# The second norm's row from VectorE to ScalarE, routing one to three steps earlier, constant tables over four steps

## What is computed

```python
# attention: 16 heads of 8, keys and values from ctx, queries from layernorm(x)
x = x + tanh(g_xattn) * attention(layernorm(ctx), layernorm(layernorm(x)))
# experts: 8 routed of which 2 are taken for a token, and 1 shared, F = 256
xn = (x - mean(x)) / sqrt(var(x) + 1e-5)          # the second norm
gates = sigmoid(xn @ Wg)
vals, idx = top_k(gates, 2); vals /= vals.sum()
shared = (silu(xn @ Ws1) * (xn @ Ws3)) @ Ws2
routed = sum over the two experts e of vals * (silu(xn @ We1[e]) * (xn @ We3[e])) @ We2[e]
x = x + tanh(g_ffn) * (shared + routed) / 3
```

## Time and profile before

| | |
|---|---|
| median of three runs | 461.3 us (459.54 to 461.4) |
| profiled execution | 458.93 us, span 457.1 us |
| TensorE busy | 359.4 us (79%) |
| VectorE busy | 344.0 us (75%) |
| ScalarE busy | 264.9 us (58%) |
| GpSimd busy | 279.4 us (61%) |
| mean granted clock of TensorE | 0.915 of full speed |

### The profile page before, as it was taken

How to read it: one execution, slowest core, us unless ns; L and a number is a source line. 1 busy time by engine, 2 the same in 40 slices (tenths; PEclk the granted TensorE clock), 3 DMA queues, 4 the chain that set the end, 5 groups by cost and what they waited for, 6 DMA issues and landing times.

```text
span 457.1 us, 10667 instructions
## 1 busy us (share of the span) xinstructions
PE 359.4 (79%) x3718; PEld 269.3 (59%) x3718; DVE 344.0 (75%) x866; ACT 264.9 (58%) x601; POOL 279.4 (61%) x375
## 2 busy tenths in 40 slices
PE   0689999997998969899869710999999999999400
PEld 0356666665765647676658600777777777778300
DVE  2559999999999998998848820576777777777447
ACT  1257777776687746687656600355555555556244
POOL 3373666666379966888647773017777777777700
PEclk9999999999799988899979865799999999999855
DMA  4920699991001110000001155113236666541179
GB/s 110 275 77 3 261 375 377 391 385 41 13 27 49 36 48 25 27 25 26 25 23 42 49 217 165 52 52 94 93 95 231 232 231 230 210 184 52 47 264 298
DMA packets 39331, 62.36 MB, mean 136 GB/s; under 512 B 5936, under 2 KB 23344, under 8 KB 39280
## 3 DMA queue, kind: packets, MB, share of 16 engines
q1 hardware_dynamic: 32704, 51.12, 32.6%
q0 software_dynamic: 4992, 10.30, 6.7%
q10 hardware_dynamic: 1584, 0.27, 0.4%
HBM read 18.32 MB, written 31.56 MB: 109 GB/s over the span
## 4 chain that ended last, share of the span: by engine, by line
PE 41%; DVE 25%; issue 13%; POOL 13%; ACT 4%; DMA 3%; POOLq 0%; DVEq 0%; SPq 0%; ACTq 0%
POOL expert_rows L545 7%; PE ps L1215 6%; PE ps L1216 5%; PE ps L1217 5%; DVE row_max L935 5%; PE ps L1252 3%; DVE inv_sum L976 3%; PE ps L1158 3%; POOL token_sums L622 3%; PE ps L1112 3%; DVE norm L900 2%; PE ps L1240 2%; PE ps L1238 2%; PE ps L1239 2%; DVE x_sb L1061 2%
## 5 line engine op out<-in xcount | busy, mean ns | idle before, releaser
L622 POOL DMA_INDIRECT token_sums<-prob,y_at x92 | 94.5, 1027 | 60.7 <-DVE prob L1035 38.8
L545 POOL DMA_INDIRECT expert_rows<-c_sb,pos x64 | 64.3, 1005 | 16.9 <-issue 16.8
L587 POOL TENSOR_TENSOR k_mask<-k_st,head_mask 128x512 f32<-128x512 f32 x32 | 33.5, 1046 | 43.8 <-ACT k_st L695 43.6
L739 ACT ACTIVATE h_hi<-prob 128x512 fp32r<-128x512 f32 x62 | 38.3, 634 | 36.5 <-DVE prob L998 36.5
L732 ACT ACTIVATE probT<-ps 128x512 f32<-128x512 f32 x62 | 36.9, 598 | 30.6 <-PE ps L1217 27.0
L1112 PE MATMUL ps<-k_mask,qT 32*64 32x256 f32 x512 | 46.0, 431 | 9.4 <-DVE prob L941 7.7
L998 DVE TENSOR_TENSOR prob<-ps,probT 128x512 f32<-128x512 f32 x62 | 40.2, 684 | 13.9 <-ACT probT L732 10.9
L935 DVE TENSOR_REDUCE row_max<-ps 128x16 f32<-128x1024 f32 x32 | 38.9, 1216 | 11.0 <-PE ps L1112 10.9
L1003 DVE TENSOR_TENSOR h_lo<-prob,h_hi 128x512 fp32r<-128x512 f32 x62 | 40.5, 689 | 3.4 <-ACT h_hi L739 0.4
L1019 DVE TENSOR_TENSOR xT_lo<-ps,xT_hi 128x512 fp32r<-128x512 f32 x23 | 15.9, 692 | 35.9 <-ACT xT_hi L744 35.9
L703 ACT ACTIVATE probT<-ps 128x512 f32<-128x512 f32 x64 | 35.2, 595 | 10.5 <-PE ps L1158 10.4
(11 more groups left out here) (164 smaller groups left out, 977.1 us busy)
## 6 DMA issues: line engine op xcount, KB each, us to landing
expert_rows<-zeros SPq DMA_DIRECT2D x36, 520.0 KB, 5.2
c_sb<-expert_rows SPq DMA_DIRECT2D x23, 260.0 KB, 2.7
wbuf_hi<-w_hi SPq DMA_DIRECT2D x15, 384.0 KB, 2.9
wbuf_lo<-w_lo SPq DMA_DIRECT2D x15, 384.0 KB, 3.4
w_raw<-in_L_ffn_We_dram SPq DMA_DIRECT2D x24, 128.0 KB, 4.2
c_sb<-token_sums SPq DMA_DIRECT2D x8, 256.0 KB, 4.7
xT_lo<-token_sums SPq DMA_DIRECT2D x8, 256.0 KB, 4.9
out_dram<-x_sb SPq DMA_DIRECT2D x8, 256.0 KB, 4.9
```

The source lines that it names most:

```text
L545: pool.indirect_dma_start(out=xs, out_offset=bass.IndirectOffsetOnAxis(pos[:, k, i:i + 1], 0), in_=c_sb[:, i, :], in_offset=None).then_inc ...
L622: pool.indirect_dma_start(out=ys, out_offset=bass.IndirectOffsetOnAxis(y_at[:, s, k:k + 1], 0), in_=yrows[:, s % 2, k * D:(k + 1) * D], in ...
```

## The change

Four things are changed together. The normalised row of the second norm, `(x - mean) * rstd`, is made by ScalarE as `x * rstd + shift`; GpSimd makes `shift = -mean * rstd` after the power. Gates, counts and ranks of the first four groups come one to three steps earlier, and all five parts of `routing` stand in one step. Scatters begin in step 15 and not 18, and after step 37 only tiles 28 to 31 are left. The tables are made in four parts over steps 0 to 3.

```diff
-        GATE_STEP = [14, 22, 30, 34, None]
-        COUNT_STEP = [16, 24, 32, 36, None]
-        RANK_STEP = [17, 25, 33, 37, None]
+        GATE_STEP = [13, 21, 29, 33, None]
+        COUNT_STEP = [14, 22, 30, 34, None]
+        RANK_STEP = [15, 23, 31, 35, None]
...
         def scatter_tiles(t):
-            if 18 <= t < NT:
-                return range(t - 18, t - 17)
-            return {NT: [14], NT + 1: [15], NT + 2: [16, 17], NT + 3: [18, 19], NT + 4: [20, 21],
-                    NT + 5: [22, 23]}.get(t, [])
+            if 15 <= t < NT:
+                return range(t - 15, t - 14)
+            return {NT: [17, 18], NT + 1: [19, 20], NT + 2: [21, 22], NT + 3: [23, 24], NT + 4: [25, 26],
+                    NT + 5: [27]}.get(t, [])
...
-            def tables():
+            def tables(part):
+
                 exact = dict(channel_multiplier=0, allow_small_or_imprecise_dtypes=True)
+                if part == 0:
+                    pool.memset(zeros[:, :], 0.0).then_inc(zeros_set, 1)
...
+                if part == 1:
+                    pool.wait_ge(table_step, 1)
...
+                if part == 2:
+                    pool.wait_ge(table_step, 2)
...
+                if part == 3:
...
+                    pool.iota(slot_less[:, :], [[1, DYN]], base=1 - JMAX, **exact).then_inc(tables_ready, 1)
...
@@ GpSimd, step(t, b) @@
                 i = t - 4
                 if within(i):
                     pool.wait_ge(var2_done, i + 1)
+                    if reused(i):
+                        pool.wait_ge(xn2_ready, i - 1)
                     pool.tensor_tensor(rstd2[:, b:b + 1], var2_eps[:, b:b + 1], minus_half[:, 0, 0:1],
-                                       ALU.pow).then_inc(scale2_ready, 1)
+                                       ALU.pow).then_inc(rstd2_done, 1)
+                    pool.wait_ge(rstd2_done, i + 1)
+                    pool.tensor_scalar(shift2[:, b:b + 1], mv2[:, b, 0:1], rstd2[:, b:b + 1], -1.0, ALU.mult,
+                                       ALU.mult).then_inc(scale2_ready, 1)
...
-                if t == 0:
-                    tables()
+                if 0 <= t < 4:
+                    tables(t)
...
             def unit(n):
-                if n == TAIL_UNIT:
-                    for i in range(24, 28):
-                        scatter(i)
...
@@ ScalarE, step(t, b), between xT_f and w_hi @@
+                i = t - 4
+                if within(i):
+                    act.wait_ge(scale2_ready, i + 1)
+                    act.activation(c_sb[:, i, 0:D], x_sb[:, i, :], ACT.Identity, bias=shift2[:, b:b + 1],
+                                   scale=rstd2[:, b:b + 1]).then_inc(xn2_ready, 1)
...
@@ VectorE, step(t, b) @@
                 for g, last in enumerate(COUNT_STEP):
-                    if last is not None and last - 1 <= t <= last:
-                        for part in (range(0, 3) if t < last else range(3, 5)):
+                    if t == last:
+                        for part in range(5):
                             routing(g, part)
...
-                i = t - 4
-                if within(i):
-                    dve.wait_ge(scale2_ready, i + 1)
-                    dve.tensor_scalar(c_sb[:, i, 0:D], x_sb[:, i, :], mv2[:, b, 0:1], rstd2[:, b:b + 1], ALU.subtract,
-                                      ALU.mult).then_inc(xn2_ready, 1)
...
                     if reused(t - 3):
-                        dve.wait_ge(xn2_ready, t - 4)
+                        dve.wait_ge(scale2_ready, t - 4)
...
@@ TensorE, step(t, b) @@
                 i = t - 6
                 if within(i):
                     pe.wait_ge(xT_f32_ready, i + 1)
+                    pe.matmul(p_logit[:, i, :], xT_f32[:, b, :], wg_raw[:, :], start=True,
+                              stop=True).then_inc(logits_ready, 1)
                     if t > NT and t in GATE_STEP:
                         pe.wait_ge(gate_exp, GATE_STEP.index(t) + 1)
-                    pe.matmul(p_logit[:, i, :], xT_f32[:, b, :], wg_raw[:, :], start=True,
-                              stop=True).then_inc(logits_ready, 1)
...
                     if isinstance(t, int) and t == NT + 1:
                         pe.wait_ge(attn_ready, NT)
+                    if t > NT + 1 and t in RANK_STEP:
+                        pe.wait_ge(pos_ready, RANK_STEP.index(t) + 1)
                     pe.transpose(x2_bank(t), c_sb[:, i, 0:D], ident[:, :]).then_inc(xn2_turned, 1)
```

More of the change, by code:

```diff
@@ L118, in gated_attention_and_experts @@
         rstd2 = sb("rstd2", [P, 2])
+        shift2 = sb("shift2", [P, 2])
         minus_half = sb("minus_half", [P, LB, 2])
@@ L224, in gated_attention_and_experts @@
         var2_done = sem("var2_done")
+        rstd2_done = sem("rstd2_done")
         scale2_ready = sem("scale2_ready")
@@ new lines, in tables @@
+            def tables(part):
+                exact = dict(channel_multiplier=0, allow_small_or_imprecise_dtypes=True)
+                if part == 0:
+                    pool.memset(zeros[:, :], 0.0).then_inc(zeros_set, 1)
+                    pool.wait_ge(zeros_set, 1)
+                    pool.memset(zeros[:, :].rearrange("p (r d) -> p r d", d=XW)[:, :, D:D + 1], NOWHERE).then_inc(zeros_set, 1)
+                    pool.iota(c_sb[:, :, D].rearrange("p (c k) -> p c k", k=CH), [[CT, NC], [1, CH]], base=0,
+                              channel_multiplier=CH, allow_small_or_imprecise_dtypes=True).then_inc(table_step, 1)
+                if part == 1:
+                    pool.wait_ge(table_step, 1)
+                    pool.tensor_scalar(c_sb[:, :, D], c_sb[:, :, D], 1.0 / T, None, ALU.mult)
+                    pool.iota(nowhere[:, :, :], [[ROWS, SLOTS], [1, CH]], base=2 * T, channel_multiplier=CH,
+                              allow_small_or_imprecise_dtypes=True)
+                    pool.memset(ones[:, :], 1.0)
+                    pool.memset(not_before[:, :], -1.0)
+                    pool.memset(earlier[:, :, :], 1.0)
+                    for b in begins.values():
+                        pool.memset(b[:, :], 1.0)
+                    pool.iota(carry[:, 0, :], [[T // P, E]], base=0, channel_multiplier=0,
+                              allow_small_or_imprecise_dtypes=True).then_inc(table_step, 1)
+                if part == 2:
+                    pool.wait_ge(table_step, 2)
+                    pool.affine_select(out=not_before[:, :], in_=not_before[:, :], compare_op=ALU.is_ge, fill=0.0, base=0,
+                                       pattern=[[-1, P]], channel_multiplier=1)
+                    pool.affine_select(out=earlier[:, :, :], in_=earlier[:, :, :], compare_op=ALU.is_ge, fill=0.0, base=-1,
+                                       pattern=[[1, E], [-1, E]], channel_multiplier=0)
+                    for n, t in begins.items():
+                        pool.memset(t[:, :].rearrange("p (e t) -> p e t", e=E)[:, :, 0:1], 0.0)
+                if part == 3:
+                    pool.iota(steps512[:, :, :], [[T, E], [ROWS, JMAX - 1]], base=ROWS, **exact)
+                    pool.iota(slot_id[:, :], [[1, DYN]], base=0, **exact)
+                    pool.iota(slot_less[:, :], [[1, DYN]], base=1 - JMAX, **exact).then_inc(tables_ready, 1)
```

26 lines of the change are left out of this document (removed).

## The result

The changed kernel takes 475.68 us (median of 4 runs, 473.71 to 478.94) where the kernel before, on the same chip, takes 460.42 (459.1 to 461.4): a ratio of 1.034, with a 95% interval of 1.0274 to 1.0407. It is slower by 3.4%. The forecast was 464.1 us and the range ended at 470; the sign was right, the size was not, and the time lies outside the range.

A forecast was written before the change was run, and what follows sets the result against it. VectorE's loop (5.74 us) and a ScalarE-TensorE loop (5.5 us) lay close, with GpSimd's at 6.45 in scatter steps. Attention +4.9, tail +4.0 and backlog -6.1 gave +2.8 us: median 464.1 us, range 456 to 470.

The forecast's parts named there:

- fifteen steps, 13 to 28: Attention steps with the first two groups' routing and scatters: from 101.0 us to 103.4, +2.4 us.
- Two at 5.9, since GpSimd enters them ahead: Two steps after group 0's routing: 5.9 us each, GpSimd's lead hiding its longer loop; then 5.9, 6.4, 7.1.
- The merged routing: All five parts in one step: 9.9, 5.5, 7.6 us for group 0, with a slow-clock step; 10.4 for group 1.
- Nine steps, 4 to 13: Early attention steps before routing: 5.9 us each, 53.1 us in all for 51.9, +1.2 us.
- Tables: Tables in four steps end TensorE's wait before the scores at 32.21 us: gain 0.9 us, no more.
- 28 to 31: Three attention steps with group 2's routing: from 18.7 us to 20.9, +2.2 us.
- The tail: From step 31 to the last places: +4.0 us, between +2.8 and +5.1, TensorE waiting for places in step 35.
- The backlog: Scatters after the last places: only tiles 28 to 31 left, ending 6.1 us before 278.9 without delays.
- Rival 1: ScalarE's row is hidden, steps fall to VectorE's loop of 5.48 us: 455.7 us, chance 0.20.
- Rival 2: The merged routing costs nothing, slow clock covered and places in time for step 35: 457.1 us, chance 0.17.
- Rival 3: GpSimd is later than thought, shift costing 0.54 us and w_lo's wait reaching steps 15 to 25: 469 us, chance 0.18.
- Rival 4: Identity needs a table load beside Silu, two loads each in steps 33 to 35: 471.8 us, chance 0.03.

The follow-up runs named there:

- order experiment: The changed kernel with power and shift ahead of k_mask in GpSimd's step: 468.25 us, 1.0172; the order was also compared with the row alone and with routing split.
- e2_routing: The kernel before with only the earlier, merged routing, its scatters and TensorE's waits; row on VectorE, tables in one step: 473.02 us, 1.0271.
- the fillers: 28 idle identity matmuls on TensorE behind steps 14, 22 and 30, added to the kernel with the earlier, merged routing alone: 466.43 us, 1.0108.
- e1_row: The kernel before with only the ScalarE row and its shift; routing and tables as before: 467.36 us, 1.0166.
- e3_tables: The kernel before with only the tables made in four steps: 458.4 us, 0.9929.
- e6_group3_late: The earlier, merged routing alone, but with the fourth group left in its old steps, in two parts, scatters thinned to match: 470.98 us, 1.0179.
- e7_tail_scatters: The kernel before with tables in four steps and scatters of tiles 14 to 25 packed denser into steps 32 to 37: 453.98 us, 0.9813.
- e5_early_split: The earlier routing alone, with each group's parts split over two steps as before, scatters from step 16: 463.02 us, 1.0008.
- e11_tail_fillers: The kernel before with tables in four steps, denser scatters behind step 31, and 10 idle matmuls before the scores of steps 16 and 24: 455.21 us, 0.9878.

## Why the prediction was wrong

**The failed step: fifteen steps, 13 to 28, at +2.4 us.** They cost 16.5. Two of its assumptions fell.

*"Two at 5.9, since GpSimd enters them ahead", then "5.9, 6.4, 7.1", and behind group 1 "5.9, 6.2, 6.9, 6.1".* The loop itself was sized right: 7.1 us on average over four parts, 6.25 before; measured over the five from k_mask 18 to 23, 7.19 and 6.28. And k_mask to w_lo, 2.82 predicted, was 2.85. What was wrong is where it binds. From the k_mask at 124.03 on, GpSimd waits for k_st only twice in the next eleven (3.54 us behind group 1, 0.17 later), and its loop is paid every time: from k_mask 17 to k_mask 30 are 97.5 us, 86.5 before. The rows of before held the refutation: GpSimd's wait for k_st in a step without scatters is 1.44 us. That is its whole lead. A loop longer by 1.2 us than the others uses it up in about one step; I let it last for four. Besides, the lateness doesn't stay with GpSimd: the row waits for the shift, and exp, v_st, sT, tT and TensorE's k queue behind the row. The waits of 1.96, 1.44 and 1.72 us shown above are that, and behind some of them stands the lower clock. I had written "behind that w_hi" and stopped there. The order experiment prices this at 6.6 to 9.3 us by the ratios, in three settings.

*The merged routing: 9.9, 5.5 and 7.6 for group 0, then 5.9 and 5.9; 10.4 for group 1.* Group 0's three steps came at 10.7, 5.5 and 7.8, close. But these were set against steps of before that I had not added up: its five steps from 13 to 18 take 33.6 us, mine 34.8, and in `e2_routing` 38.9, since the slow step (8.8) and the next (7.2) both ran over. For group 1 the step was 14.0 us and not 10.4; in `e2_routing` 13.1. In the changed kernel two reasons show in the rows: TensorE came into it at the lower clock (157.76), and the routing operation L832 took 1.72 us at 166.79 where its twin at 165.18 took 0.22, beside a scatter and k_mask (167.36) on GpSimd, until that ended. The Trainium skill (SBUF — State Buffer, "SBUF: two separate sides") has a VectorE operation with two SBUF inputs, against a GpSimd operation that reads SBUF, among those that lock the other out or are locked out; L832 is one, and the row agrees. The twin at 165.18, beside a scatter alone (164.98), was not held. Nor is the hold new. The kernel before has one in the same group, beside a scatter and k_mask (162.97) again:

```profile
162.54 1.83 DVE L821 TENSOR_TENSOR gate_tmp<-gate_tmp,rank 128x64 f32<-128x64 f32 x1
```

With it, step 23 of before already took 10.9 us for the same three parts of the routing that step 15 did in 8.9: I priced group 1 from group 0's row when its own was there, 2 us dearer, and put 0.3 for operations held beside GpSimd. The part costs 12 us by the runs, and 7.5 of them go with the fillers: most of it is the lower clock in a step that has nothing to cover it. I named that mechanism and gave it 1.0 us a group.

**Nine steps, 4 to 13.** Predicted +1.2; steps 7 to 13 came at 5.9 to 6.0 us with VectorE idle 0.54. But step 6 took 7.6 us in this run (5.4 or 6.0 in the other kernels with the row), so the stretch was 54.7 us for 51.9. It is one more place of the lower clock, behind a gap of 1.00 us that ended when tT did:

```profile
48.35 0.58 PE L1155 MATMUL ps<-sT,wk_sb 128*128 128x128 f32 x2 [1.00 <-issue]
48.73 1.91 PE L1166 MATMUL ps<-ident,prob 128*128 128x128 f32 x8
```

In `e1_row` the stretch was 53.2 us, for 53.1 in the forecast. ScalarE's row adds 0.40 us to its loop (0.36 taken), and GpSimd's shift 0.26 to 0.38 (0.30 taken).

**Tables.** Predicted -0.9, measured -2.3 at step 4 and -3.3 by the ratio of `e3_tables`. Term mis-sized: I stopped the gain at the gap before the scores, but step 2 as a whole came down from 7.8 to 5.9 us.

**28 to 31.** +2.2 predicted, +2.4 measured.

**The tail.** TensorE was to go on at 30.3 us after the start of step 31: it did at 30.4 (265.83 less 235.41), behind a wait of 3.74 us for the places. The rest of the term was off: the exchange was to give back 1.6 us and the lower clock to take up to 2.3, of which I put about half in. The twelve rows of chunk 3's up-projections, most at 0.63 instead of 0.39 us, took 4.9 us where before they took 2.8, so the clock took 2.1; with TensorE's +4.5 that leaves 0.8 given back and not 1.6. The term is +5.8, not +4.0, above its upper bound of 5.1. `e6_group3_late` shows that this is group 3's move.

**The backlog.** -6.1 predicted, -7.1 measured. The term was mis-sized by one scatter: the row at 277.62 in the earlier trace rows is the last but one of the 28, and the 278.9 that the prediction took for the end of before is where the last one starts:

```profile
278.89 0.95 POOL L545 DMA_INDIRECT expert_rows<-c_sb,pos  x1 [0.30 <-issue]
```

With its end at 280.1 the same working gives -7.4, near what came, and a forecast 1.3 us lower: this slip hid a part of the miss. Most of the gain comes without the moves, in `e7_tail_scatters` (-5.0).

**The rest.** Taken as unchanged; it was 2.0 us longer in the profiled run; the experiments have 177.1 to 180.2. These are single executions, and the cause is open.

**The rivals.** Rival 1 (the row hidden) falls in the early steps, at 5.97 us. With power first the row's whole cost can't be told from none in one setting, is 3.6 us in another. Rival 2 falls: the merge costs 12 us. Rival 3 (GpSimd later than I think) had the right place and the right sign, with too small a price, 5 us over the forecast, and a shift of 0.54 us where it takes 0.26 to 0.38. Rival 4 falls: six table loads before, six after. The signs that the prediction named as right were there (one routing step at 14.0 and not near 10), and none of its signs of being wrong: they tested whether each mechanism is in place, and not in how many steps it sets the pace.

## What to carry to other kernels

An engine's wait in the steps before a change is the whole of its lead; compare it with what the new work adds per step, and charge the longer loop from the step in which the lead is used up. Follow a late result through the whole queue of the engine that waits for it, to the next wait on it: here two operations of 128x1, placed behind one of 1.05 us instead of ahead of it, cost 1.4 to 2.0% because ScalarE's row, and behind it five operations and TensorE, stood still for them. And don't merge small VectorE work into one block ahead of what TensorE waits for: in one step it cost 12 us more than split over two, more than half of it TensorE's clock. Last, ask of each part of a change what it gives alone: spreading the tables and packing the scatters denser (`e7_tail_scatters`) gained 1.9%, more than any kernel here that also moved the routing.

## What the hardware showed that I had not expected

- TensorE's granted clock was at its lower level behind waits of 1.44 us (157.76) and 1.00 us (48.35), yet a wait of 1.96 us (129.07) was followed by k at full speed (0.49 us), and a gap of 2.51 us ahead of 107.65 in `e5_early_split` by scores at full speed (0.66 us), with the lower clock only 3 us later. From the gap alone the fall can't be told.
- Idle matmuls in a gap gave back 7.5 and 7.8 us where nothing covers the slow step. In `e11_tail_fillers`, where other work does, they gave nothing, and the lower clock came a step later.
- A VectorE operation of 0.22 us took 1.72 beside a scatter and k_mask on GpSimd (1.83 before).
- ScalarE's Identity with a scale and a bias per partition, 128x128 from SBUF to SBUF, takes 0.49 us and lets the next operation start after 0.40.
